# Dummy products on TensorE ahead of the first maximum-row wait of four attentions

## What is computed

```python
x = L0(x, ctx)    # 16 heads of 16: causal self attention and context keys, softmax, then a feed-forward part
x = L1(x, ctx)    # three layers, 4 heads of 64: first with context keys, then two self attentions, softmax
x = L2(x, ctx, idx)  # squared-relu attention in a window of three context tokens
x = L3(ctx, ctx, x, mask)  # 16 heads of 16 over context keys, softmax, then a feed-forward part
scores = einsum(q, k); attn = softmax(scores); out = einsum(attn, v)
```

## Time and profile before

| | us |
|---|---|
| median of three runs | 1718.94 |
| the three runs | 1711.73, 1718.94, 1720.42 |
| the profiled execution, its own time | 1712.14 |
| its span in the profile | 1710.4 |

### The profile page before, as it was taken

One profiled execution on the slowest core, in us unless ns is written; L12 is line 12 of the kernel. 1 busy time (PEld: TensorE's weight loads), 2 busy tenths in 40 slices (PEclk: granted clock), 3 DMA queues, 4 the chain that ended last, 5 costly groups with the idle time before them and its releaser, 6 DMA issues. The chain is left out here.

```text
span 1710.4 us, 23183 instructions
## 1 busy us (share of the span) xinstructions
PE 1394.2 (82%) x7755; PEld 813.7 (48%) x7755; DVE 1032.1 (60%) x2390; ACT 755.2 (44%) x1058; POOL 518.1 (30%) x330
## 2 busy tenths in 40 slices
PE   5857999899849978788999839799996678487897
PEld 3523344344338856543344326344442567244796
DVE  6657777677264346756566147575553766676754
ACT  5312555455766544532333434233333633344564
POOL 4000000000041033215777921068776346100312
PEclk9859999999979988988999968799998789799998
DMA  6960333330000000274312203633300000650001
GB/s 234 256 133 2 53 53 53 54 53 2 14 13 1 1 1 21 89 223 88 84 42 61 92 1 136 197 87 87 87 25 25 1 1 1 146 102 12 1 1 49
DMA packets 78175, 110.40 MB, mean 65 GB/s; under 512 B 16431, under 2 KB 55529, under 8 KB 76265
## 3 DMA queue, kind: packets, MB, share of 16 engines
q1 hardware_dynamic: 78057, 108.91, 25.6%
HBM read 70.55 MB, written 37.80 MB: 63 GB/s over the span
## 5 line engine op out<-in xcount | busy, mean ns | idle before, releaser
L1216 ACT ACTIVATE x_feat<-banks,key_bias 128x1024 f32<-128x1024 f32 x160 | 176.5, 1115 | 272.5 <-PE banks L1122 196.4
L1044 POOL TENSOR_TENSOR x_feat<-x_feat 128x1024 f32<-128x1024 f32 x112 | 265.8, 2373 | 67.3 <-ACT x_feat L1216 54.7
L1077 PE MATMUL banks<-stacks 128*128 128x512 f32 (+4 forms) x640 | 235.7, 408 | 34.7 <-DVE max_parts L1240 13.4
L1216 ACT ACTIVATE x_feat<-banks 128x1024 f32<-128x1024 f32 (+3 forms) x224 | 180.7, 839 | 164.4 <-PE banks L1116 107.9
L1137 PE MATMUL banks<-x_feat,v_group 128*64 128x512 f32 (+4 forms) x1312 | 229.5, 564 | 11.5 <-ACT x_feat L1216 10.8
L1246 DVE TENSOR_REDUCE max_parts<-banks 128x1 f32<-128x512 f32 (+3 forms) x384 | 191.6, 552 | 40.8 <-PE banks L1077 24.3
L1077 PEld LDWEIGHTS banks<-stacks 96*128 96x128 bf16 (+1 forms) x640 | 85.5, 141 | 201.2 <-DVE max_parts L1240 93.4
L1376 POOL TENSOR_TENSOR stacks<-w_even,stacks 128x512 fp32r<-128x512 f32 x16 | 21.9, 1400 | 495.6 <-ACT stacks L1368 495.6
L1113 PE MATMUL banks<-stacks 99*128 99x512 bf16 (+3 forms) x512 | 141.7, 350 | 22.2 <-DMA stacks<-neg_max_parts 13.5
L1240 DVE CUSTOM_DVE_ANT_0 scratch<-banks,mask_rows 128x512 f32<-128x512 f32 x128 | 88.3, 690 | 55.5 <-PE banks L1077 55.2
L1121 PE MATMUL banks<-stacks 128*128 128x512 f32 x256 | 110.3, 431 | 9.4 <-DMA stacks<-neg_max_parts_r 9.4
(11 more groups left out here) (267 smaller groups left out, 2483.5 us busy)
## 6 DMA issues: line engine op xcount, KB each, us to landing
stacks<-q_parts_r SPq DMA_DIRECT2D x24, 512.0 KB, 8.2
stacks<-k_parts_r SPq DMA_DIRECT2D x24, 512.0 KB, 10.8
q_parts_r<-stacks SPq DMA_DIRECT2D x16, 512.0 KB, 2.8
k_parts_r<-stacks SPq DMA_DIRECT2D x16, 512.0 KB, 4.3
v_group<-v SPq DMA_DIRECT2D x14, 512.0 KB, 14.8
q_parts<-y_tok SPq DMA_DIRECT2D x16, 384.0 KB, 6.0
stacks<-q_parts SPq DMA_DIRECT2D x16, 384.0 KB, 5.2
w_even<-in_w SPq DMA_DIRECT2D x4, 1024.0 KB, 6.7
```

Source lines behind the costliest of these rows:

```text
L1044: e.tensor_tensor(total, total, p, ALU.add)
L1077: m = e.matmul(PS[:, bank, at:at + wide], q[0:rows, h, qt * P:(qt + 1) * P], keys[0:rows, h, k0:k0 + wide], start=True, stop=not diag, ski ...
L1216: e.activation(dst, PS[:, 2 * (st % 2):2 * (st % 2) + 2, 0:CH - t.q0], ACT.Exp, scale=A.scale, bias=bias).then_inc(s.p_ready, 1)
```

## The change

Just ahead of the wait for the maximum rows of the first group (r = 0), TensorE makes 20 products in L0 and 10 in each of the other three attentions. They multiply real operands of the first group (a piece of its keys by the first 512 queries of its first head) and write bank 5, which nobody reads before it is written anew. They change no semaphore. No other engine's stream changes.

```diff
+        def keep_busy(n):
+            if A.dh == 16:
+                q, k = slot16(A, 0)
+                k0, wide = (P, P) if A.self else (0, SC)
+                left, right = k[0:K16, 0, k0:k0 + wide], q[0:K16, 0, 0:CH]
+            else:
+                wide = P
+                qa, qb, ka, kb = slot64(A, 0)
+                left, right = ka[:, 0, 0:P], qa[:, 0, 0:CH]
+            for _ in range(n):
+                e.matmul(PS[0:wide, 5, :], left, right, start=True, stop=True, skip_group_check=True)
...
             if A.self and A.dh == 64:
                 e.wait_ge(s.loaded[slot_of(A, r) + 2], (r // A.slots + 1) * 48)
+            if r == 0 and not A.window:
+                keep_busy(20 if A.dh == 16 and A.self else 10)
             if A.halved and r == 0:
                 e.wait_ge(s.first_rows, 16 * A.parts * A.nh)
             elif not A.window:
```

## The result

The change makes the kernel slower, by less than 2%. In twenty runs of each kernel the median went from 1714.42 us (1706.29 to 1720.44) to 1720.95 us (1713.13 to 1728.78). The ratio is 1.0040, with a 95% interval of 1.0025 to 1.0056; on 1714.42 us that is +6.9 us (+4.3 to +9.6). The profiled execution took 1718.18 us, with a span of 1716.4 us and a mean granted clock of 0.912, the same clock as before.

A forecast was written before the change was run, and what follows sets the result against it. TensorE, busy for 82% of the span, and its clock were taken to bound the kernel. Terms 0 (L0) - 2.4 (L1) + 1.8 (L3) = -0.6 us gave 1711.5 for the profiled execution, 1718.3 us as median; range 1710 to 1724.

The forecast's parts named there:

- Start 777.53 + 0.37 = 777.90: L1, second layer: the ten products start at 777.90, when the turn of the maxima (L1085) ends.
- ahead of 782.60 by 0.40 us: L1, second layer: ten products of 0.43 us end at 782.20, 0.40 us before the first score at 782.60.
- the won 1.2 us per layer: L1: first scores run at the high clock, so each of two layers wins 1.2 us, 2.4 us in all.
- L0: 0 us: L0: twenty products fit inside the wait and the clock is lost again before the work, so 0 us.
- the case of 6.66: L0: if the clock rises after 6.66 us, at 112.5, TensorE is idle from 113.5, for 2.9 us.
- the clock holds: Rival: in L0 the high clock lasts behind the wait, winning up to 3.85 us, time 1714.5; chance 0.16.
- L3: +1.8 us: L3: ten products take 2.2 us at the high clock, 0.4 of it hidden in the wait, costing 1.8 us.
- The weight loads hide: All places: loads run beside products, costing nothing; the rival that they don't gave 1727.7 us, chance 0.04.
- The late clock: Rival: the clock answers later, so L3 pays +3.9 us and L1 wins nothing, time 1722.8; chance 0.13.
- The change does nothing: Rival: products nobody reads are left out on the way to the chip, time 1718.9, no new rows; chance 0.03.
- a net of -3 to +2.5 us: Whole kernel: the main forecast's band for the net effect, given chance 0.64.
- the 4.5 and the 3.9 us: Range: down 4.5 us if the clock holds in L0, up 3.9 us if the clock is late in L3.

The follow-up runs named there:

- e1: Kernel before plus ten products in each of the two L1 layers at the change's place, none in L0 and L3: ratio 1.0027, median 1717.31 us.
- e5: Kernel before plus ten products per L1 layer at the end of the stage before, ahead of the meeting, none elsewhere: ratio 0.9984, median 1712.58 us.
- e10: Kernel before plus 36 products in L0, ten per L1 layer ahead of the meeting, none in L3: ratio 0.9951, median 1705.48 us.
- e2: Kernel before plus the twenty products in L0 alone: ratio 0.9998, median 1714.23 us.
- the controls: Profiles of kernels whose stage in question is left as before; end of L0 at 356.1 to 361.0 us in eight profiles, median 359.2.
- e6: Kernel before plus 36 products in L0 at the change's place, none elsewhere: ratio 0.9979, median 1712.14 us.
- e3: Kernel before plus the ten products in L3 alone: ratio 1.0026, median 1719.07 us.
- e4: Kernel before plus seven products per L1 layer at the end of the stage before, ahead of the meeting, none elsewhere: ratio 1.0020, median 1718.44 us.
- e7: Kernel before with the split of the maxima reading one input from PSUM, no new products: ratio 0.9984, median 1712.24 us.
- e8: Kernel before with the split out of PSUM and seven products per L1 layer ahead of the meeting: ratio 0.9975, median 1712.28 us.
- e11: Kernel before with 36 products in L0, ten per L1 layer ahead of the meeting, and the split out of PSUM: ratio 0.9958, median 1708.08 us.

## Why the prediction was wrong

The median was forecast at 1718.3, 0.6 us below the one given, and the range of 1710 to 1724 holds the 1720.95 measured. That is luck: the forecast stood on a median of three runs (1718.94) that lies 4.5 us above the one of twenty (1714.42), and this hid most of the error. The sign and the size are wrong: +6.9 us against the kernel before in the same comparison, outside what such a measurement leaves to chance.

- **The step that failed** is the first sentence on L1: "Start 777.53 + 0.37 = 777.90". They started at the meeting's end, 4.10 us behind the end of L1085, and not at its end. The wait that the working laid them into was for the most part one that they can't be in. All that follows from it fell too: "ahead of 782.60 by 0.40 us" became 3.84 us late at the first score, and the won 1.2 us per layer became a loss of 3.2 and 2.3 us at the third group's L1085, 3.3 and 2.7 in e1 (+4.6 us by its ratio, where -2.4 stood). I read the wait of 4.70 us in the earlier trace rows as one wait for one DMA. It was two, one behind the other, the meeting of L263 and then the DMA, and the row names only the last. The products stand between the two.
- **The mechanism in L1 was right**: with the products ahead of the meeting the clock is high for the first scores, and the first value product comes 1.13 to 1.16 us sooner (e5), for which the working had 1.2; e10 has 9.35 and 9.36, the same.
- **L0: 0 us was right**, and for its reason. The clock rose after 6.2 us, near the case of 6.66, the products ended at 112.95 and the pause was 3.32 us (2.9 in that case), longer than the 2.70 that had taken the clock before; e2 has 0.9998 (0.9975 to 1.0020), which leaves room for some 4 us to either side, and an end of L0 within the controls. What the rival "the clock holds" had as its price, 3.85 us, is near what is really there, 3.2 us at the first value product, but only for products that last as long as the wait (e6).
- **L3: +1.8 us was right in mechanism and near in size.** The products outlasted the landing of the rows by 1.7 us in the change and by 1.3 in e3. Two errors of the working went against each other. The cover was 0.8 us in both and not 0.40, since the time between TensorE's last chunk and the landing differs between profiles: in six of the eleven controls TensorE doesn't wait there at all, in the other five 0.2 to 0.9 us. And in the change the products began before the clock had risen, so that ten took 2.49 us (granted clock 0.87) and not 2.2.
- **The weight loads hide**: the products follow one another in 0.44 and 0.22 us with a load for each (ten in the 4.43 us from 781.33 to 785.76 at the low clock; ten from 1506.29 to 1508.45 in L3 of e3, at 1.00). The Trainium skill, "TensorE: Matmul & The Clock Gate", section "Part 3: Packing small matmuls", says that weights load beside a running product only where the row groups differ; this is not borne out here either, as all ten loads use the same rows as the products beside them. The same section names a background weight buffer as another way for a load to go ahead, which would fit.
- **The late clock** wasn't what decided. In L3 the clock rose 6.55 us behind L1085, against 6.34 before; the products had only begun sooner. In L1 it was up 4.2 us behind the first product in one layer, and 6.0 us in the other, after the scores had begun. "The change does nothing" is refuted by the 50 new products.
- The sum by measured terms: 0 + 4.6 + 4.5 = 9.1 us by the ratios of e1 to e3, or 0 + 3.2 + 2.3 + 1.7 = 7.2 by the distances of the change itself (third L1085 in L1, delay behind the landing in L3), against +6.9 (+4.3 to +9.6) for the whole. Both lie in that interval.
- **The chances**: 0.64 went to a net of -3 to +2.5 us, which is not what came, and no rival had the products start late. "Within 0.5%" had 0.90, and the 0.4% measured lies inside it, but by luck: it was argued from gains, and the loss of L1 was in no term. The bounds of the range take the 4.5 and the 3.9 us off 1718.3, though both count from 1718.94, which moves them by some 0.6 us.

## What to carry to other kernels

A row of idle time names only what came last. Before work is put into a wait, read where in the engine's own program the wait stands, and what else it passes there: a meeting of all engines, or an engine that comes to it late, can take up most of the wait, and then the work belongs ahead of the meeting. Work made to keep the clock must last until close to the landing of what is awaited; where it ended 3.3 us early in L0 (20 of 36 products) or 1.7 to 1.9 us early in L1 (e4) the clock fell again and nothing was won. Where it starts late, it costs its length. And what is changed at one point moves the phase of what follows, so read the next groups too.

## What the runs showed of the hardware

- A VectorE operation on 16x128 elements took 0.28 us, and 1.91 to 2.12 us when it began in the midst of a GpSimd operation of 2.37 us, both with their inputs in SBUF. With one input from PSUM it took 0.28 us in all ten groups (e7, e8, e11).
- In L0, the first group's work (mostly bf16, 96 and 99 rows) kept TensorE busy for 18.02 of 19.13 us and the granted clock stayed at 0.50 (1.2 GHz); the same work that began at 1.00 (2.4 GHz) kept 1.00 for all of 19.25 us (e6). In L3 of e6 it stayed at 0.50 with TensorE busy for 9.94 of 9.94 us. The Trainium skill, "TensorE: Matmul & The Clock Gate", section "Why this matters for your kernels", lets continuous work get the fast clock; these stretches don't agree with it.
- After pauses of 1.72 and 1.89 us (e4) and in one layer of two after 1.55 us (e8), the clock stayed at 1.00 for another 1.2 to 2.0 us of dense scores and then was at 0.50 for 3.4 us, though TensorE was busy throughout. In the other layer of e8, after a pause as long, and after pauses of 0.8 to 1.0 us (the third layer of e10, both of e11), it stayed up. So the length of the pause alone didn't decide it.
